# Indirect transfers of a sampling and mixture-of-experts kernel, issued four at a time with a wait for each group to land

## The reference, cut to what matters

```python
h = tok(x)                       # [32, 1024, 64]: per image 32x32 queries, each samples 8 points
h = concatenate([h, txt], 1)     # [32, 1152, 64]
h = h + causal_attention(layernorm(h))
h = h + top2_moe(layernorm(h))   # 16 experts, hidden 128

def tok(fm):                     # fm [32, 64, 128, 128]
    q_feat  = bilinear_sample(fm, grid)              # fixed 32x32 grid
    offsets = gelu(layer_norm(q_feat @ W_o1)) @ W_o2 * 4
    sampled = bilinear_sample(fm, grid + offsets)    # data dependent: 8 points a query, 4 corners each
    k, v    = sampled @ W_k.T, sampled @ W_v.T
    return softmax(q . k over the 8 points) applied to v

def top2_moe(x):
    w, e = top2(x @ gate_w + gate_b); w = softmax(w)
    y = x + sum_k w_k * (relu(x @ w1[e_k] + b1[e_k]) @ w2[e_k] + b2[e_k])
    return layernorm(y) * gamma + beta
```

## Time and profile before

| | us |
|---|---|
| time, median of 3 | 4563.92 |
| time, lowest and highest | 4560.54, 5620.5 |
| span of the profiled execution | 6851.9 |
| busy in it: PE / DVE / ACT / POOL | 4265.1 / 3165.0 / 2222.4 / 3077.1 |

### The profile page before, as it was taken

One profiled execution on the slowest core, in us unless ns is written; L12 is line 12 of the kernel. 1 busy time (PEld: TensorE's weight loads), 2 busy tenths in 40 slices (PEclk: granted clock), 3 DMA queues, 4 the chain that ended last, 5 costly groups with the idle time before them and its releaser, 6 DMA issues.

```text
span 6851.9 us, 83914 instructions
## 1 busy us (share of the span) xinstructions
PE 4265.1 (62%) x26592; PEld 3681.7 (54%) x26592; DVE 3165.0 (46%) x10220; ACT 2222.4 (32%) x5378; POOL 3077.1 (45%) x3089
## 2 busy tenths in 40 slices
PE   3566765657566575665766667565765757656664
PEld 2555655646455464654656556454654646545543
DVE  1455445354454534545354544534545454544521
ACT  1333332323333332332333323333333333322321
POOL 2554454444534445354454544445344444545331
PEclk9777777777767776786777767777777777767765
DMA  6754443635536354353545536254353545433122
GB/s 194 216 154 136 145 135 115 177 96 157 148 103 189 86 174 119 118 165 94 175 118 160 144 106 190 84 176 119 118 164 93 175 113 152 138 106 89 54 59 67
DMA packets 938637, 911.33 MB, mean 133 GB/s; under 512 B 121306, under 2 KB 822362, under 8 KB 938072
## 3 DMA queue, kind: packets, MB, share of 16 engines
q1 hardware_dynamic: 805768, 598.22, 30.0%
q0 software_dynamic: 132432, 307.74, 15.5%
HBM read 583.69 MB, written 323.53 MB: 132 GB/s over the span
## 4 chain that ended last, share of the span: by engine, by line
another core or an unknown queue 31%; PE 29%; DVE 14%; issue 13%; ACT 10%; SPq 1%; DMA 1%; POOL 0%; DVEq 0%; POOLq 0%; ACTq 0%
PE ps L867 4%; PE ps L881 4%; PE ps L1024 3%; PE ps L1032 3%; PE ps L812 3%; PE ps L964 3%; PE ps L942 2%; ACT rows L1048 2%; ACT xm L1128 2%; DVE prod L1229 1%; PE ps L954 1%; PE ps L1006 1%; PE ps L823 1%; ACT kv_sb L1048 1%
## 5 line engine op out<-in xcount | busy, mean ns | idle before, releaser
L758 POOL DMA_INDIRECT gath<-table,idx x2048 | 2048.2, 1000 | 2909.6 <-issue 1211.3
L881 PE MATMUL ps<-w_kv,samp_t 128*128 128x128 f32 x4096 | 702.9, 323 | 166.6 <-issue 88.1
L867 PE MATMUL ps<-const,prod 128*128 128x128 f32 x4096 | 684.4, 322 | 168.8 <-issue 81.7
L964 PE MATMUL ps<-v_sb,probs_t 128*128 128x64 f32 x2880 | 455.2, 307 | 476.9 <-issue 223.1
L881 PEld LDWEIGHTS ps<-w_kv,samp_t 128*128 128x128 f32 x4096 | 637.0, 234 | 201.0 <-issue 130.5
L964 PEld LDWEIGHTS ps<-v_sb,probs_t 128*128 128x128 f32 x2880 | 442.9, 229 | 544.2 <-issue 303.5
L867 PEld LDWEIGHTS ps<-const,prod 128*128 128x128 f32 x4096 | 596.5, 172 | 202.7 <-issue 152.4
L774 POOL DMA_INDIRECT xs_d<-xm,row x512 | 525.9, 1027 | 392.7 <-DVE row L1229 231.6
L790 POOL DMA_INDIRECT ya<-ys_d,row x512 | 493.4, 964 | 454.4 <-DMA ys_d<-yx 268.6
L1229 DVE TENSOR_TENSOR prod<-gath,corner_w 128x1024 f32<-128x1024 f32 x512 | 619.9, 1219 | 159.3 <-remote 70.6
L942 PE MATMUL ps<-k_t,q_t 128*128 128x512 f32 (+3 forms) x960 | 479.7, 592 | 181.6 <-ACT v_sb L1048 76.5
(11 more groups left out here) (171 smaller groups left out, 6593.0 us busy)
## 6 DMA issues: line engine op xcount, KB each, us to landing
table<-rows SPq DMA_DIRECT2D x224, 1024.0 KB
fm<-in_x SPq DMA_DIRECT2D x256, 512.0 KB
wx<-w_d SPq DMA_DIRECT2D x768, 128.0 KB
gath<-table,idx POOLq DMA_INDIRECT x2048
wx<-w_d SPq DMA_DIRECT2D x64, 512.0 KB
table<-rows SPq DMA_DIRECT2D x32, 960.0 KB
xg<-xs_d SPq DMA_DIRECT2D x192, 130.0 KB
ys_d<-yx SPq DMA_DIRECT2D x192, 128.0 KB
```

Source lines behind the costliest of these rows:

```text
L758: pool.indirect_dma_start(out=gath[:, n % NG, p, :], out_offset=None, in_=tables[par], in_offset=bass.IndirectOffsetOnAxis(ap=idx[:, par, ...
L867: last = pe.matmul(bank(0, p * P, p * P + P), prod[h][:, (p * 2 + dx) * P:(p * 2 + dx + 1) * P], ident, is_transpose=True, start=(dx == 0) ...
L881: last = pe.matmul(bank(1, p * P, p * P + P), samp_t[n % 2][:, (4 * h + p) * P:(4 * h + p + 1) * P], w_kv[:], start=True, stop=True)
L964: last = pe.matmul(bank(7, (i % 8) * C, (i % 8) * C + C), probs_t[n % 3][:, (k % 4) * P:(k % 4) * P + P], v_sb[:, k, :], start=(k == 0), s ...
```

## The change

A constant `AT_ONCE = 4` is added, and three waits, all on GpSimd:
- gather: ahead of every tile but a pair's first, POOL waits until tile n-1 has landed in full; between the 4th and the 5th transfer of every tile it waits until the first four have landed;
- scatter: after every 4 of the 32 it waits until all so far have landed;
- fetch: after every 4 of the 16 it waits likewise.

No transfer is added, removed, resized or moved in any engine's order.

```diff
+AT_ONCE = 4
@@ gather
                 for h in range(2):
                     pool.wait_ge(*wcorn[h].rise(pair, n + 1 - NG))
                 pool.sem_inc(pool_gate, 1)
+                if n:
+                    pool.wait_ge(*gath_in[(n - 1) % NG].rise(pair, 16 * NP_ * ((n - 1) // NG + 1)))
                 for p in range(NP_):
+                    if p == AT_ONCE:
+                        pool.wait_ge(*gath_in[n % NG].rise(pair, 16 * (NP_ * (n // NG) + AT_ONCE)))
                     k = (t * 2 + b) * NP_ + p
                     pool.indirect_dma_start(
                         out=gath[:, n % NG, p, :], out_offset=None, in_=tables[par],
@@ scatter
                     pool.sem_inc(pool_gate, 1)
+                if j and j % AT_ONCE == 0:
+                    pool.wait_ge(*scattered.rise(pair, 16 * j))
                 pool.indirect_dma_start(
                     out=xs_d[par], out_offset=bass.IndirectOffsetOnAxis(ap=row[:, par, j:j + 1], axis=0),
@@ fetch
                     pool.sem_inc(pool_gate, 1)
+                if j and j % AT_ONCE == 0:
+                    pool.wait_ge(*fetched.rise(pair, 16 * (KT * QT_N * b + j)))
                 n = k * SLOTS + b * QT_N + t
```

## The result

The changed kernel takes 6211.49 us (median of four, 6188.15 to 6216.15) beside 4569.76 us of the kernel before: 1.3585 times as long, 95% interval 1.3551 to 1.3619. It is slower, inside the range of 5200 to 6400, and 361 us above the 5850 that were predicted.

The account below looks back on a forecast made before the run. POOL, which issues the transfers, was to become the bound: 3840 (issues) + 1690 (waits) + 110 (front) + 198 (stops in the last stretch) + 18 (behind the last fetch) = 5856, predicted as 5850 us, range 5200 to 6400.

Parts of the forecast that it names:

- POOL becomes the bound: In the loop, POOL needs 346 us a period against some 283 for the others, so DVE, PE and ACT wait for gathers.
- issues with their 0.30 us gaps: All 3072 POOL transfers, with starts 1.25 us apart: 3840 us of POOL's time.
- front: POOL's time at the program's start, before the first gather: 122.8 us profiled, put at 110 us.
- stops for others: POOL's stops in the last stretch of the program: 298 us profiled, scaled to 198 us.
- The size of one wait: Each added POOL wait: landing plus restart less the 0.30 us gap, taken as 2.4 us, 704 times, 1690 us.
- The room of 27 us a period: POOL's spare time in the unprofiled loop before the change: 398 us over 15 periods, about 90% occupied, not yet the bound.
- The assumption on the unexplained 31%: Chain stops without known releaser, some 2124 us, are mostly missing from unprofiled executions; without them the span would be 4728 us.
- Hidden waits: Rival: POOL's added waits are hidden and the time stays at 4560 to 4650 us; chance 0.05.
- The gap of 0.30 us as the profiler's: Rival: POOL's gap between issues exists only under profiling, issues take 2918 us, time about 5000 us; chance 0.13.
- Landing under load dominating: Rival: each POOL wait costs 3.2 us, giving 6419 us, or 6500 with some idle time; chance 0.10.
- Faster, because less is in flight: Rival: grouped transfers leave room for SyncE's loads; at most 4495 us, under 2%; chance of over 2% faster 0.02.
- A period: POOL's time for one period of the loop with the waits: 346 us against 240 before.

Follow-up runs that it names:

- the runs one group late: Changed kernel with gather waits only, each for the four gathers before the last four: 7051 us beside 7025 of the kernel before, 6997 beside 6954.
- the breaks: Kernel before, POOL writing a scratch tile and waiting for that write after every 4th transfer: one write 4807 us, three writes 5059 us, beside 4567.
- the gather waits alone: Changed kernel without its scatter and fetch waits: 6394 us beside 7025 of the kernel before, ratio 0.9095.
- groups of eight: Changed kernel with AT_ONCE = 8 instead of 4: 6366 us beside 7025 of the kernel before, ratio 0.9066.
- the short break: Kernel before, POOL writing one scratch tile and waiting for that write after every 4th transfer: 4807 us beside 4567, 6673 beside 6943.

## Why the prediction was right, and where it was off

**POOL becomes the bound: right.** It was the whole sum, and the rows after show it term by term. The terms, as predicted and as measured in the changed kernel:

| term | predicted | measured |
|---|---|---|
| issues with their 0.30 us gaps | 3840 | 2141.3 + 497.9 + 544.4 + 922 = 4106 |
| waits, less the gap | 1690 | 1504.9 + 239.6 + 184.7 - 666 x 0.30 = 1729 |
| front | 110 | 122 |
| stops for others | 198 | 187.3 + 20.7 + 10.4 = 218 |
| behind the last fetch | 18 | 18 |

The measured column adds up to 6193 of the span of 6210; 10 more are POOL's own setup transfers.

**The size of one wait: right on average, by parts not.** 2.4 us was taken, less the gap; it is 1729/704 = 2.46. Quiet, it is 2.05 - 0.30 = 1.75, within the bounds read from the earlier trace rows. The mean gather wait is 3.29 - 0.30 = 2.99, more than I took; fetches, at 2.20, and scatters, at 1.35, are cheaper. That these come out at 2.46 together is in part luck. So is the place near the upper end, which I chose because a wait would end POOL's readiness for the next transfer: a passed wait ends nothing, as the runs one group late show. By the Trainium skill's 2.3 us (DMA: Bandwidth & Descriptors, "Anatomy of one DMA — SWDGE (gpsimd) path") the sum of the waits was estimated at 1619; the runs show 1729.

**The term that was mis-sized is the issues, by 266 us,** three quarters of the 361 that are missing. I wrote that the means of the earlier trace rows are "a little above" and went on with 1.25 us from three rows. The means give 2048.2 + 525.9 + 493.4 + 922 = 3990 us for the kernel before, 150 more. The other 116 are issues that got longer (1046 ns after 1000, 1063 after 1027). Where a sum is wanted, the mean over the 3072 instructions goes in, not the duration of a typical one.

**The room of 27 us a period: wrong,** in the same way: with 3990 us of issues and 340 at the ends only some 240 us are left at 4570, and the breaks speak against even these being room. It did no harm to the sum, since that was built from POOL's own parts, but "it isn't yet the bound" was wrong.

**The assumption on the unexplained 31%: wrong in its reason, right in its use.** I took the stops for something of the profiled execution. In three of five comparisons they come in every execution. That 6852 less 31% came near the unprofiled median was luck, since that share also hangs on which records a trace lacks. And it was luck that the comparison fell on a chip of the first kind: on the other the sum would have met 6205 us too, but as a gain of 11% where a loss of 28% was forecast. The step that followed from it, that the profiled execution's span may grow to some 6900 to 7300 us, failed: it is 6210, on either kind, because with the added waits there are no stops, which nothing in the sum allowed for.

**The rivals.** Hidden waits: no, on a chip without stops; a difference of 36%. The gap of 0.30 us as the profiler's: no, the profiled execution of the changed kernel (6212 us, 922 of them such gaps) is as long as the three others (6188 to 6216). Landing under load dominating: the wait was 2.46, not 3.2 us. "Faster, because less is in flight" was given 0.02 and priced by the 1% of DMA in the chain. For the comparison that was asked it didn't happen; beside the kernel before of 6943 us the direction of it did, at 11%, though hardly less is in flight, and the price came from the stops, which I had named only as a condition.

**A period.** 346 us predicted. A tile's two waits cost more than thought, and with gathers issued every 1.35 us the loop's period is (5846.9 - 122.2)/16 = 358 us on average, the lighter first pairs included (first and last gather start of the changed kernel).

## What to carry to other kernels

An engine that only issues transfers has to be summed like any other: count times mean, gaps included, against the time, since idle time in a longer profiled execution isn't room. A wait for a group of transfers costs its landing and the restart, less the gap: about 1.7 us quiet and 3.0 on average for gathers here, on an issuing engine that is the bound. A wait that lies one group back has passed before it is reached and adds no idle time. And where a third of the chain has no releaser, time the kernel on more than one chip before calling a throttle of transfers a loss or a gain.

## What was not expected

The same program takes 4567 to 4570 us on some chips and 6943 to 7025 on others. In the slower case compute engines stop for 10 to 30 us at a time, as between 142 and 179 us above, while POOL goes on issuing every 1.25 us and ACT takes up a result that PE had finished at 140.97 us only at 157.06. On such chips the kernel whose every group of four lands before the next had no share of the chain without a releaser (0%), the gather waits alone had 19%, groups of eight 26%, the short break 27%, and kernels without a break 30 to 32%. What holds the engines up, and what differs between the chips, stays open.
